# A relational layer's one-hot marks: sixteen short VectorE instructions per iteration, or two long ones made an iteration ahead

## The reference

```python
def _rgcn_layer(h, src, dst, et, W, root_w, b, N):
    xw = jnp.einsum('ni,rio->rno', h, W)
    cnt = jnp.zeros((W.shape[0], N), h.dtype).at[et, dst].add(1.0)
    msg = xw[et, src] / cnt[et, dst][:, None]
    agg = jax.ops.segment_sum(msg, dst, num_segments=N)
    return agg + h @ root_w + b
...
for l in range(hop):
    W = jnp.einsum('rb,bio->rio', comp[l], bases[l])
    h = _rgcn_layer(out, src, dst, et, W, root[l], bias[l], N)
    h = jnp.maximum(h, 0.0) if l < hop - 1 else h
    out = SELF_WEIGHT * out + (1.0 - SELF_WEIGHT) * h
```

## Time and profile before

| | |
|---|---|
| Median of 3 timed runs | 5106.49 us (5106.47 to 5111.46) |
| Span of the profiled execution | 5889.7 us |
| Busy of that span: PE, DVE, ACT, POOL | 59%, 40%, 23%, 38% |
| Mean granted clock of PE | 0.726 of full speed |
| Gathers of the relational passes | 1664, 1574.4 us of POOL busy |

### The profile page before, as it was taken

The page is one execution under the profiler, slowest core; times in us unless marked ns, Lnnn a source line. Parts: engine busy times, 40 slices in busy tenths (PEclk is TensorE's granted clock), DMA queues, the critical chain, the costliest instruction groups (busy, mean ns, idle before and its releaser), DMA issues.

```text
span 5889.7 us, 68338 instructions
## 1 busy us (share of the span) xinstructions
PE 3488.8 (59%) x18857; PEld 2347.3 (40%) x18858; DVE 2346.7 (40%) x6053; ACT 1356.1 (23%) x2994; POOL 2262.0 (38%) x2340
## 2 busy tenths in 40 slices
PE   5599996998633334333333333337995566566566
PEld 3255553444422223222232332333444455445445
DVE  7756566114322222222122222223116555555556
ACT  2555451001200000000000000001003555555555
POOL 3000001000366666665666666661002444444442
PEclk8699998999756665666555555557996677777767
DMA  2111113222522222222111111113220222122112
GB/s 70 52 68 46 67 45 130 92 87 91 156 56 69 66 68 65 65 69 66 45 46 45 45 45 46 46 43 121 87 109 16 43 45 44 41 43 45 45 41 57
DMA packets 264711, 371.66 MB, mean 63 GB/s; under 512 B 63251, under 2 KB 200250, under 8 KB 256298
## 3 DMA queue, kind: packets, MB, share of 16 engines
q1 hardware_dynamic: 186790, 251.51, 12.8%
q0 software_dynamic: 74464, 114.31, 8.5%
q10 hardware_dynamic: 3364, 4.69, 0.3%
HBM read 261.10 MB, written 109.21 MB: 63 GB/s over the span
## 4 chain that ended last, share of the span: by engine, by line
PE 21%; issue 17%; another core or an unknown queue 13%; DVE 8%; POOL 8%; DVEq 6%; DMA 1%; ACT 1%; ACTq 0%; POOLq 0%; SPq 0%
POOL GS L719 8%; PE psum L1375 7%; PE psum L1535 5%; DVEq L1877 3%; DVE GS L1877 3%; PE psum L1321 3%; PE psum L1562 2%; DMA GS<-xw_table,stage 1%; DVEq L1884 1%; PE psum L1468 1%; PE psum L1469 1%; PE psum L1529 1%; PE psum L1300 1%; DVE O L2514 0%
## 5 line engine op out<-in xcount | busy, mean ns | idle before, releaser
L719 POOL DMA_INDIRECT GS<-xw_table,stage x1664 | 1574.4, 946 | 1444.9 <-issue 1075.0
L1375 PE MATMUL psum<-HA,HT 128*128 128x512 fp8e4 (+1 forms) x5733 | 1251.5, 369 | 54.2 <-DVE HT L2060 54.2
L1321 PE MATMUL psum<-GS 128*128 128x96 f32 x3328 | 688.6, 383 | 652.7 <-DMA GS<-xw_table,stage 576.6
L1321 PEld LDWEIGHTS psum<-GS 128*128 128x128 f32 x3328 | 635.2, 289 | 701.6 <-issue 698.2
L719 POOL DMA_INDIRECT HA<-p_table,stage x624 | 602.1, 965 | 734.4 <-ACT stage L1085 509.2
L1375 PEld LDWEIGHTS psum<-HA,HT 128*128 128x128 bf16 x5733 | 554.0, 100 | 632.5 <-DVE HT L2060 55.2
L1877 DVE TENSOR_SCALAR GS<-iota,HT,wt 128x96 f32<-128x96 f32 x1680 | 473.4, 348 | 454.9 <-issue 453.3
L1891 DVE TENSOR_TENSOR HA<-HA,psum 128x96 f32 x208 | 52.8, 254 | 1388.2 <-remote 964.7
L1300 PE MATMUL psum<-Wcat,HT 128*128 128x512 f32 x196 | 177.1, 1057 | 459.9 <-DVE HT L2349 410.7
L1039 ACT ACTIVATE HA<-psum 128x392 fp8e4<-128x392 f32 x784 | 349.4, 494 | 344.0 <-PE psum L1280 331.2
L815 ACT ACTIVATE stage<-edge_cols 128x16 int32 (+1 forms) x104 | 22.2, 216 | 1551.1 <-PE psum L1321 693.6
(11 more groups left out here) (383 smaller groups left out, 4221.3 us busy)
## 6 DMA issues: line engine op xcount, KB each, us to landing
HT<-dst_rows SPq DMA_DIRECT2D x212, 256.0 KB
xw_table<-HT SPq DMA_DIRECT2D x100, 512.0 KB, 3.2
HA<-adj SPq DMA_DIRECT2D x26, 1600.0 KB, 6.4
adj<-HA SPq DMA_DIRECT2D x13, 3136.0 KB, 9.5
HA<-adj SPq DMA_DIRECT2D x26, 1536.0 KB, 9.7
GS<-xw_table,stage POOLq DMA_INDIRECT x1664
HA<-p_table,stage POOLq DMA_INDIRECT x624
h_table<-HA SPq DMA_DIRECT2D x4, 960.0 KB, 5.6
```

The source lines that it names most:

```text
L719: nc.gpsimd.indirect_dma_start(out=to, out_offset=None, in_=table, in_offset=bass.IndirectOffsetOnAxis(ap=idx, axis=0)).then_inc(done, 16)
L1321: last = nc.tensor.matmul(bank[h][:, 0:WINDOW], G3[g][:, j, :], S_pair[h][:, t, :], start=(t == 0), stop=(t == 2 * GT - 1))
L1375: last = nc.tensor.matmul(bank[s][:, 0:w], Hs4[:, b, t, :], adj_tile[s][:, b * GW:b * GW + w], start=(b == 0 and t == 0), stop=(b == SRCS ...
```

## The change

The sixteen marks of an iteration are made by two DVE instructions on [128, 16, 96]: a comparison of `iota` with `dl_pair`, both read through broadcast patterns, and a multiplication in place by `wt`, with a wait for the first on the same engine between them. They go to one of two buffers `S_turn` of 16 marks each, which lie in `HT` (columns 4096 to 7167, behind the four staging places of the block's products and ahead of `hop_sum` and `dl_pair`). The marks of iteration it + 1 are issued at the start of iteration `it`, before both adds. PE waits for them once, at the start of its iteration. The loops of both engines take two iterations a turn, so that the buffer is known (`in_turns`), with the first six written out. Since marks and adds don't change what a block needs, the sixth check of `flags` states that a group's block is never `LAG` iterations behind the group: it flags `g - 4 * lo >= 4 * LAG`.

```diff
--- before.py
+++ after.py
@@ -144,7 +144,8 @@
         G3 = [t.rearrange("p (j f) -> p j f", f=P) for t in G]
         S = GS[:, 4 * GT * P:]
         S3 = [S[:, i * GT * 2 * P:(i + 1) * GT * 2 * P].rearrange("p (j d) -> p j d", d=2 * P) for i in range(2)]
-        S_pair = [S[:, i * 2 * GT * WINDOW:(i + 1) * 2 * GT * WINDOW].rearrange("p (j d) -> p j d", d=WINDOW) for i in range(2)]
+        S_turn = [HT[:, 4 * R * P + i * 4 * GT * WINDOW:4 * R * P + (i + 1) * 4 * GT * WINDOW].rearrange("p (j d) -> p j d", d=WINDOW)
+                  for i in range(2)]
         dst_b = [tail[:, i * GT * P:(i + 1) * GT * P].bitcast(I32) for i in range(2)]
         agg_s = [GS[:, i * GW:(i + 1) * GW] for i in range(2)]
         own_s = [GS[:, (2 + i) * GW:(3 + i) * GW] for i in range(2)]
@@ -472,6 +473,14 @@
             for g in range(10, DENSE):
                 body(g, g % 2, g // 2)
 
+        def in_turns(eng, body):
+
+            for it in range(LAG + 1):
+                body(it, it % 2, it - LAG if it >= LAG else None)
+            with eng.Fori((LAG + 1) // 2, ITERS // 2) as i2:
+                for u in range(2):
+                    body(i2 * 2 + u, u, i2 * 2 + (u - LAG))
+
         def in_fours(eng, body, steps):
 
 
@@ -1308,26 +1317,24 @@
 
             def sum_pass(l, of_block):
 
-                def iteration(it, block):
+                def iteration(it, s, block):
+                    pe.wait_ge(windows_ready, ((ITERS + 1) * l + it + 1) * 2)
+                    pe.sem_inc(pe_turn, 1)
                     for h in range(2):
                         k = it * 2 + h
-                        pe.wait_ge(windows_ready, (PAIRS + 1) * l + k + 1)
                         pe.wait_ge(sums_added, PAIRS * l + k + 1)
                         for g in (2 * h, 2 * h + 1):
                             pe.wait_ge(gathered[g], 64 * (ITERS * l + it + 1))
                             pe.sem_inc(pe_turn, 1)
                             for j in range(GT):
                                 t = (g % 2) * GT + j
-                                last = nc.tensor.matmul(bank[h][:, 0:WINDOW], G3[g][:, j, :], S_pair[h][:, t, :],
+                                last = nc.tensor.matmul(bank[h][:, 0:WINDOW], G3[g][:, j, :], S_turn[s][:, g * GT + j, :],
                                                         start=(t == 0), stop=(t == 2 * GT - 1))
                             last.then_inc(windows_summed, 1)
                         if h == 0 and block is not None:
                             of_block(block)
 
-                with pe.Fori(0, LAG) as it:
-                    iteration(it, None)
-                with pe.Fori(LAG, ITERS) as it:
-                    iteration(it, it - LAG)
+                in_turns(pe, iteration)
                 for b in range(IN_PASS, HOP_BLOCKS):
                     of_block(b)
 
@@ -1872,19 +1879,21 @@
 
             def sum_pass(l, beside):
 
-                def windows(k, s):
-                    for j in range(2 * GT):
-                        last = V.tensor_scalar(S_pair[s][:, j, :], iota[:, 0:WINDOW], dl_pair[:, bass.ds(k * 2 * GT + j, 1)],
-                                               wt[:, bass.ds(k * 2 * GT + j, 1)], ALU.is_equal, ALU.mult)
-                    last.then_inc(windows_ready, 1)
+                def windows(it, s):
+
+                    spread = lambda t: t[:, bass.ds(it * L16, L16)].unsqueeze(2).broadcast_to([P, L16, WINDOW])
+                    V.tensor_tensor(S_turn[s], iota[:, 0:WINDOW].unsqueeze(1).broadcast_to([P, L16, WINDOW]), spread(dl_pair),
+                                    ALU.is_equal).then_inc(windows_ready, 1)
+                    dve.wait_ge(windows_ready, ((ITERS + 1) * l + it) * 2 + 1)
+                    V.tensor_tensor(S_turn[s], S_turn[s], spread(wt), ALU.mult).then_inc(windows_ready, 1)
 
                 windows(0, 0)
 
-                def iteration(it, block):
+                def iteration(it, s, block):
                     at = [dve.value_load(pair_i[0:1, bass.ds(it * 2 + h, 1)], min_val=0, max_val=TRASH_COL) for h in range(2)]
+                    windows(it + 1, 1 - s)
                     for h in range(2):
                         k = it * 2 + h
-                        windows(k + 1, 1 - h)
                         dve.wait_ge(windows_summed, GROUPS * l + 2 * k + 2 + CREDIT)
                         dve.wait_ge(sums_added, PAIRS * l + k + 2)
                         to = A[:, bass.ds(at[h], WINDOW)]
@@ -1892,10 +1901,7 @@
                         if block is not None:
                             beside[h](block)
 
-                with dve.Fori(0, LAG) as it:
-                    iteration(it, None)
-                with dve.Fori(LAG, ITERS) as it:
-                    iteration(it, it - LAG)
+                in_turns(dve, iteration)
                 dve.wait_ge(sums_added, PAIRS * (l + 1) + 2)
                 for b in range(IN_PASS, HOP_BLOCKS):
                     for step in beside:
@@ -2261,7 +2267,10 @@
                 ch(V.tensor_tensor(hi_pair, hi_pair, lo_pair[:, :], ALU.subtract))
                 ch(V.tensor_scalar(hi_pair, hi_pair, float(WINDOW), None, ALU.is_ge))
                 top(4, hi_pair[:, 0:PAIRS])
-                ch(V.reduce_max(two_flags[:, 0:1], flag1[:, 0:5], AX.X))
+                ch(V.scalar_tensor_tensor(of_group, lo, -4.0, iota[:, 0:GROUPS], ALU.mult, ALU.add))
+                ch(V.tensor_scalar(of_group, of_group, 4.0 * LAG, None, ALU.is_ge))
+                top(5, of_group)
+                ch(V.reduce_max(two_flags[:, 0:1], flag1[:, 0:6], AX.X))
 
             def needs_rest():
```

## The result

| | before | after |
|---|---|---|
| Median of 4 timed runs each | 5107.84 us | 5280.32 us (5279.15 to 5284.09) |
| Ratio, 95% interval | | 1.0338 [1.0326, 1.0351] |
| Profiled execution: time, span | 5889.7 (span) | 5280.65, 5278.7 |

What follows compares the result with a forecast made beforehand. The prediction took POOL's gathers to bound both passes at 20.0 us an iteration. Its terms summed as 5106.5 + 165 (held gathers) + 1 (sixth check) - 2 (marks removed) = 5270.6, so 5271 us, range 5100 to 5340.

Steps and rivals of the forecast that it cites:

- POOL bounds the passes at 20.0 us: Both relational passes: in the timed runs POOL's sixteen gathers, one every 1.25 us, set 20.0 us an iteration.
- at least 288 of their 348 us: Both passes: of 348 us excess in the profile, at least 288 are absent from timed runs, leaving at most 60.
- Marks removed, -2 us: Passes: sixteen short DVE instructions fewer per iteration save POOL's gathers about 2 us in all.
- Two instructions of 1.76 us: DVE in each iteration: the two 128x1536 instructions take 1.76 us each, 3.6 us as a pair.
- The hold, 1.59 us an iteration, 165 us: Passes: gathers starting beside the two long instructions wait 1.59 us an iteration, 165 us over 104 iterations.
- held twice as long: Rival for the passes: a held gather doesn't get in between the two instructions, 295 us, 5401 us; chance 0.08.
- Nothing hides it: Passes: POOL is late by the hold in every iteration; at most 60 us of remaining stall may absorb some.
- POOL isn't the bound: Rival for the passes: descriptor work ignores the instructions, or a stall absorbs the delay; 5105 us, no change, chance 0.12.
- a bound elsewhere than in POOL: Sign of a wrong forecast in the passes: gather mean stays 0.946 us, or long gathers without a slower timed run.
- The sixth check, +1.1 us: Preparation: three chained DVE instructions on 208 columns at 0.37 us each add 1.1 us.
- Marks an iteration ahead, no cost: Passes: making marks a whole iteration ahead costs nothing; TensorE's four waits for marks, 10.5 us, may go.
- faster: Rival for the passes: two DVE instructions instead of sixteen remove delay before adds, at most 60 us, 5046; chance 0.09.

Runs made afterwards that it cites:

- before_again: The kernel before, unchanged and profiled anew on a chip of the kind that was timed: 5109.83 us.
- short_ahead: The changed kernel with its new order and buffers, but sixteen short mark instructions again instead of the two long ones: 5112.81 us against 5111.14, ratio 1.0003.
- both_psum: The changed kernel with one input of each long instruction (iota, wt) read from PSUM: 5112.55 us against 5111.14, ratio 1.0002.
- compare_psum: The changed kernel with iota in PSUM for the comparison alone, run twice: 5829.56 us against 5850.07 and 5841.43 against 5848.48 for the kernel before.
- extra_two_inputs: The kernel before plus one unread 128x1536 comparison with two SBUF inputs per iteration, run three times: ratios 1.0003, 1.0015 and 1.001.
- split_in_8: The changed kernel with each long instruction cut into four of 128x384, eight in all: 5180.25 us against 5111.14, ratio 1.0136.

## Why the prediction was right, step by step

**POOL bounds the passes at 20.0 us: right, by a wrong step.** The windows of `before_again` have 1040.3 us for 52 iterations. But the step "so 783.2 us exist only in the profile" was false. The unchanged kernel's own time and span differ by 1.9 us; the other 782 go with the chip. That the sum "at least 288 of their 348 us" gave the truth about the timed runs was luck: it compared executions on two kinds of chip as if they were one. Between the two profiles of before, first to last gather start has 2452.5 us against 2098.7, 354 us more, and what follows has 425 more. What those chips do for 3 us in each iteration is open; no run looked for the cause. It was also wrong to set aside the Trainium skill's rule on the gap ("Runtime: NRT & Kernel Launch", section "The ~15µs preamble/postamble breakdown") for the 783 us, which were no gap within one execution. The rule says that a profile's total lies about 6.2 us above the reported time of the same kernel, whatever the kernel. The spans here, from first to last instruction, lie 1.9 us below the time of their own execution: the gap is small, as the rule has it, but its size and side can't be compared with a total that no run here gives.

**Marks removed, -2 us: not seen.** The gathers' busy time is 1572.2 us with the short marks in the old order (`before_again`), 1575.0 with them in the new one (`short_ahead`), and 1574.0 without them and without a hold (`both_psum`). No gain shows, and at most 1.3 us were there to be had.

**Two instructions of 1.76 us: right**, 1.758 and 1.757. The gap between them is 0.14 us (2504.90 - 2503.00 - 1.76), not 0.07, so the pair takes 3.66.

**The hold, 1.59 us an iteration, 165 us: right in mechanism and size.** The trace has 1.62 and 168.5, so the forecast's whole error of 8 us lies in some 3.5 us of hold, the 2 us of marks and a few us outside the passes. `both_psum` takes the second SBUF input away and the whole loss goes; `short_ahead` takes the instructions away and it goes too; the extra instruction in the kernel before brings one hold of 0.95 to 1.02 us. The two waits in the rows are 1.48 and 0.65, forecast as 1.01 in the mean and 0.58: the second is longer by the wider gap, 0.07. That a held gather gets in between the two was right as well; the rival "held twice as long" would need gathers of up to 0.945 + 3.4 us, and the longest is 2.52. What the step left out is the second kind of hold, by one-input instructions; the preparation had it in view (the gathers at 88.14 and 89.58). In the passes the only instructions of that kind are short, so it cost the forecast nothing that can be seen.

**Nothing hides it: right on the timed chips only.** The rival "POOL isn't the bound" is just what the chips with stalls show. It was priced with a budget of 60 us; there it had some 350 and swallowed everything. Long gathers without a slower run were the prediction's own sign of a bound elsewhere than in POOL, and on those chips the gathers' busy time does not set the pass. The remark that the profile's span "may even fall" came true there, 5880.8 against 5889.7, but the kernel before spreads over 5875 to 5905 us on that chip, so the fall is not clear of it.

**The sixth check, +1.1 us: its work right, its place wrong.** In after it is

```profile
94.93 0.38 DVE L2270 SCALAR_TENSOR_TENSOR HA<-lo_g,iota 128x208 f32<-128x208 f32 x1
95.34 0.43 DVE L2271 TENSOR_SCALAR HA<-HA 128x208 f32<-128x208 f32 x1
95.80 0.37 DVE L2250 TENSOR_REDUCE HA<-HA 128x1 f32<-128x208 f32 x1
```

1.3 us with the gaps. But the first gather of the passes starts at 1547.7 instead of 1547.4, and in `short_ahead` and `both_psum`, which have the check too, at 1545.1 and 1545.6: the 1.1 us do not show behind the preparation.

**Marks an iteration ahead, no cost: right.** PE waits for them nowhere in after (7 times, 11.7 us, in `before_again`; the earlier trace rows had 4), and `short_ahead` is level with before.

**The rival "faster"** supposed that fewer DVE issues shorten a crawl. On the timed chips there is no crawl. On the others, after is at 0.9983 [0.997, 0.9996] and `compare_psum` at 0.996 and 0.9987, so a gain of a few us may be there; it is too near the noise to be called shown.

**The rule weighed.** The Trainium skill ("SBUF — State Buffer", section "Who interferes with whom") says that a DVE instruction with two SBUF inputs contends with a GpSimd one that reads SBUF, and that one with at most one SBUF input does not, unless it runs in a two-port mode. The long instructions agree with both halves: a gather takes 2.42 us beside two SBUF inputs and 0.95 beside one and PSUM. The extra copy has one SBUF input and did hold gathers (0.39 us an iteration), so the exception can't be left out; no run shows in which mode it ran. The page's inference that tensor_tensor does not hold the descriptor work does not carry over to a gather as a whole: 168.5 us of hold.

## What to carry to other kernels

When GpSimd issues indirect gathers without a break and sets the pace, look at every DVE instruction beside it by its inputs, not by its busy time: here 3.5 us of DVE with two SBUF inputs cost 1.62 us of POOL in each iteration, and the same work with one input in PSUM, or sixteen short instructions on a column of scalars, cost nothing. One input is no safe conduct by itself: a long copy inside SBUF held gathers too. If such an instruction is needed, cut it short, since a gather waits at most for the one that is running (holds of 1.62, 1.03 and 0.70 us an iteration with two, four and eight pieces; in time, 69 us with eight instead of 173 with two), or put it where the other engine is idle.

Before concluding from a gap between a profile and the timed runs, find out whether they are of the same chip: here one profile stood 782 us above another of the same kernel, and the same change cost 3.4% on chips of one kind and nothing on a chip of the other.

## What the runs showed of the hardware

- **A gather meets DVE at two moments.** Beside the long two-input instructions only its start matters: all 65 that were under way when a comparison began (0.01 to 0.94 us old) took 0.94 to 0.96 us. Beside the copy there is a second moment. Of the gathers that had begun before a copy, those begun 0.05 to 0.51 us before it ended 0.12 us after the copy (1.13 to 1.59 us long); those begun 0.53 to 0.69 us before kept 0.94 while the copy took 1.03 to 1.20 us instead of 0.96; and those begun 0.77 us or more before met nothing. So the gather needs something that the copy takes between about 0.52 and 0.77 us of its 0.945. The marks of the unchanged kernel meet it too (`before_again`): of 185 that began 0.45 to 0.60 us after a gather, 184 took over 0.37 us, up to 0.53, and of 464 that began in a gather's first 0.40 us none took over 0.33. That this is the writing of its descriptors is my reading, not shown.
- **At a near tie the gather can win.** In the kernel with the extra comparison (`extra_two_inputs`), four gathers are recorded as beginning 0.01 to 0.04 us after it and kept 0.94, and the comparison took 1.80 to 1.83 us instead of 1.76. In after, where none began less than 0.06 us behind the comparison, every one was held.
- **A copy out of PSUM held no gather that started beside it**: beside the one of 128x512 out of PSUM (0.68 us, unchanged kernel) nine of the eleven gathers that began during it took 0.94 us; the other two, 0.98 and 1.00, ran into the copy inside SBUF that follows it.
- **Records of short DVE instructions overlap**: 0.553 us each, but four in 2.00 us (`split_in_8`). The distance between their starts, not the recorded length, gives what a row of them takes. A waiting gather still goes by the recorded end: it ends 0.80 to 0.84 us after it, as beside the long ones.
